# A graph layer with linear attention and a mixture of experts: tokens sent to tiles of their experts, heads computed for two blocks at once, selves and query softmax moved into the first pass, 28 dense sets in place of 12

## The chip, the cores and the metric

The kernel runs on one NeuronCore of one Trainium2 chip. The metric is the device time of one execution in microseconds, the median of several. Engines: TensorE (PE in the profile, PEld its weight loads), VectorE (DVE), ScalarE (ACT), GpSimd (POOL), and the sync engine (SP), which here only issues DMAs.

## The reference

6250 nodes with 256 features, 200,000 edges sorted by destination. `xn` is the layer norm of `x`. Then, per node:

```
neigh = mean of xn[src] over the edges that end at the node
g     = relu([xn, neigh] @ gnn_W + gnn_b); g = g / max(|g|, 1e-12)
q,k,v = xn @ Wqkv, 8 heads of 32; q = softmax over a head's 32 features, k = softmax over all nodes
mix   = layernorm((q * scale) @ (k^T v) @ Wout) * gamma
x     = x + g + mix
tokens = layernorm(x)
x     = x + tokens + sum over the 2 best of 8 experts: weight * (gelu(tokens @ w1[e] + b1[e]) @ w2[e] + b2[e])
```

The two weights are the softmax of the router's logits, scaled to sum to one. All products but the one over the edges are in float32.

## The kernel before

The nodes are 49 blocks of 128 rows. Edges are tiles of 128, and as they are sorted by destination, tile j belongs to nodes near 4j.

**Two ways to sum over edges.** (1) Gathered tiles: GpSimd fetches the 128 source rows of a tile by an indirect DMA (L609) from a table in DRAM that holds each normalized row as two float16 halves, high and low. VectorE compares destination numbers to make a one-hot (L1273), and PE multiplies it by both halves (L653, L655). 16 tiles form a zone of 128 nodes; its sum is copied by ScalarE (L968), turned by PE (L662) and added by VectorE into `sums` (L1363). There is a ring of 24 gathered tiles. (2) Dense sets: a set is 11 groups of two tiles. PE builds, from two one-hots per tile (source row within a block; 11 destinations x 49 blocks, in two halves), a piece of the adjacency matrix (`build_group`, L687); ScalarE copies it out (L979); then PE multiplies the matrix by the table's rows, which are resident in SBUF (`multiply`, L697 and L699: 49 blocks, two matmuls of 121 weight columns each). Before, 12 sets take 264 tiles this way, and 1299 tiles are gathered.

**Stages.** At the start layer norm statistics, the table and the edges' numbers. First pass (`b1`, 49 units): per block the normalized rows are turned, stored to DRAM, and multiplied to keys and values (L761), which go to DRAM; each unit also has 4 gathered tiles and a share of the dense work. Second pass (`b2`): per block the exponentials of the keys and the context sum (L789), 3 gathered tiles, dense work. A bridge of 16 tiles turns the context into one matrix `w_mix`. Main stage: 49 blocks x 8 experts = 392 steps, with 2.6 gathered tiles per step. In a block's eight steps PE does `up` (L867) and `down` (L878) for each expert on all 128 tokens; ScalarE the Gelu (L1039); VectorE adds each expert's output times its combine weight, which is zero for six of eight (L1531). In the same steps the head of the next block runs: `project` (L805, selves and queries), the query softmax (VectorE and ScalarE, L1424 to L1436), `mix` (L832, L835), then on VectorE a chain of small operations (norms, variances, an inverse square root by Newton steps, L1105 to L1115) up to the tokens, then the routing.

**What sets the order.** Each engine's program is written out by hand from one list of units and steps (`plan_b`, `main_steps`); semaphores couple the engines. `use_order` numbers every use of the PSUM bank `turned`, which most stages share, and its uses follow one another. `plan_b` spreads the dense pieces over the units by a cost in microseconds (0.46 per group built, 0.23 per block multiplied) and a budget per unit. SP's queue holds all plain DMAs in program order, GpSimd's queue all gathers.

## Time and profile before

| | |
|---|---|
| timed, median of 3 runs | 1843.76 us (1841.33 to 1844.39) |
| span of the profiled execution | 2433.1 us |
| granted TensorE clock, mean | 0.908 |
| PE / weight loads busy | 76% / 60% |
| DVE / ACT / POOL busy | 50% / 28% / 53% |
| DMA | 251.14 MB, mean 103 GB/s |

The profile has no time of the profiled execution other than its span, which is well above the timed runs. Busy time of PE is the union of matmul records, whose ends are modelled. "Idle before" is the time that an engine stood still ahead of a group of instructions, with what ended it.

### The profile page before, as it was taken

Reading aid. Unit: us, or ns where it says so; the run is one execution under the profiler, and the core shown is the slowest. Engines: PE = TensorE matmul, PEld = TensorE weight load, DVE = VectorE, ACT = ScalarE, POOL = GpSimd, SP = SyncE. Lnnn points to the kernel's source line nnn. Section 1 sums busy time; section 2 is a strip of 40 time slices with the busy share of each in tenths; the row PEclk is TensorE's granted clock in tenths of the full one; section 3 lists DMA queues with packets and bytes.
Section 4 is the critical chain, followed back from the end, with each engine's and each line's share of the span. In section 5 each row is a group of like instructions: output and inputs, shape, how many; then the busy total and the mean of one; then the engine's idle time right before and its main releaser. Section 6 shows DMA issues by size and latency. Waiting matters only on the chain.

```text
span 2433.1 us, 34393 instructions
## 1 busy us (share of the span) xinstructions
PE 1851.1 (76%) x11044; PEld 1449.7 (60%) x11044; DVE 1222.2 (50%) x4533; ACT 685.0 (28%) x1736; POOL 1277.6 (53%) x1310
## 2 busy tenths in 40 slices
PE   0578877878748787787887787877778777777888
PEld 0355555666526665666666666666666666666677
DVE  8322222442235555455555555555555555555576
ACT  6333333332202222222222222222222222222233
POOL 1655565464655654655555555655555555545510
PEclk9899999998868988988989998988998989988999
DMA  7445554443642332322332332332332322322310
GB/s 256 140 147 158 161 158 142 121 118 106 183 120 79 98 94 66 100 77 85 98 89 80 90 94 83 94 89 76 91 92 84 90 85 85 90 81 84 92 42 13
DMA packets 144715, 251.14 MB, mean 103 GB/s; under 512 B 28046, under 2 KB 96062, under 8 KB 144542
## 3 DMA queue, kind: packets, MB, share of 16 engines
q0 software_dynamic: 62352, 170.35, 24.6%
q1 hardware_dynamic: 82190, 78.59, 10.1%
q8 instruction: 95, 1.56, 0.3%
q14 instruction: 78, 0.64, 0.1%
HBM read 216.74 MB, written 32.09 MB: 102 GB/s over the span
## 4 chain that ended last, share of the span: by engine, by line
PE 47%; another core or an unknown queue 22%; DVE 11%; issue 11%; ACT 8%; DMA 1%; SPq 1%; POOL 0%; DVEq 0%; POOLq 0%; ACTq 0%
PE ps_hidden L867 9%; PE ps_expert L878 9%; PE ps_zone L653 3%; PE ps_zone L655 3%; PE ps_proj L832 3%; PE ps_proj L805 2%; PE ps_proj L835 2%; ACT sb_stage L1039 2%; PE ps_zone L697 2%; PE ps_turned L662 2%; PE ps_zone L699 2%; PE ps_hidden L761 2%; PE ps_proj L761 2%; PE ps_expert L687 1%
## 5 line engine op out<-in xcount | busy, mean ns | idle before, releaser
L609 POOL DMA_INDIRECT sb_ring<-xn_table,sb_idx x1299 | 1270.1, 978 | 1050.4 <-PE ps_zone L655 485.3
L878 PE MATMUL ps_expert<-sb_arena,sb_stage 128*128 128x256 f32 x1568 | 444.7, 408 | 61.4 <-DVE sb_arena L1531 34.0
L1039 ACT ACTIVATE sb_stage<-ps_hidden,sb_b_col 128x128 f32<-128x128 f32 x784 | 241.7, 365 | 874.3 <-remote 469.1
L867 PE MATMUL ps_hidden<-sb_arena 128*128 128x128 f32 x3136 | 458.5, 293 | 27.7 <-ACT sb_stage L1039 21.0
L867 PEld LDWEIGHTS ps_hidden<-sb_arena 128*128 128x128 f32 x3136 | 415.8, 206 | 64.6 <-issue 30.7
L1531 DVE SCALAR_TENSOR_TENSOR sb_arena<-ps_expert,sb_small,sb_arena 128x256 f32<-128x256 f32 x392 | 189.0, 482 | 337.1 <-remote 211.6
L653 PE MATMUL ps_zone<-sb_ring,sb_onehot 128*128 128x256 f16 x1299 | 336.6, 287 | 22.6 <-issue 12.4
L878 PEld LDWEIGHTS ps_expert<-sb_arena,sb_stage 128*128 128x128 f32 x1568 | 287.4, 204 | 99.5 <-issue 58.3
L655 PE MATMUL ps_zone<-sb_ring,sb_onehot 128*128 128x257 f16 x1299 | 337.1, 288 | 6.2 <-issue 6.2
L655 PEld LDWEIGHTS ps_zone<-sb_ring,sb_onehot 128*128 128x128 f16 x1299 | 133.5, 103 | 62.6 <-issue 19.3
L653 PEld LDWEIGHTS ps_zone<-sb_ring,sb_onehot 128*128 128x128 f16 x1299 | 134.6, 104 | 51.5 <-issue 14.5
L697 PE MATMUL ps_zone<-sb_arena,sb_adjacency 128*121 128x256 f16 x588 | 147.0, 288 | 15.3 <-issue 10.9
L1273 DVE TENSOR_TENSOR sb_onehot<-sb_iota,sb_rel 128x512 f16<-128x512 f16 (+1 forms) x325 | 136.4, 420 | 34.2 <-PE ps_zone L655 24.6
L699 PE MATMUL ps_zone<-sb_arena,sb_adjacency 128*121 128x257 f16 x588 | 146.2, 287 | 9.3 <-issue 9.2
L832 PE MATMUL ps_proj<-sb_w_nb,sb_sums 128*128 128x256 f32 x196 | 77.7, 536 | 95.7 <-ACT sb_stage L1029 87.6
L832 PEld LDWEIGHTS ps_proj<-sb_w_nb,sb_sums 128*128 128x128 f32 x196 | 45.6, 257 | 112.3 <-ACT sb_stage L1029 96.4
L697 PEld LDWEIGHTS ps_zone<-sb_arena,sb_adjacency 128*121 128x121 f16 x588 | 84.3, 143 | 32.4 <-issue 25.7
L1363 DVE TENSOR_TENSOR sb_sums<-ps_turned,sb_sums 128x256 f32<-128x256 f32 x82 | 34.4, 419 | 133.9 <-PE ps_turned L662 105.6
L805 PE MATMUL ps_proj<-sb_w_aq,sb_arena 128*128 128x512 f32 x196 | 97.2, 620 | 0.0
L699 PEld LDWEIGHTS ps_zone<-sb_arena,sb_adjacency 128*121 128x121 f16 x588 | 84.3, 143 | 15.8 <-issue 15.6
L662 PE MATMUL ps_turned<-sb_consts,sb_arena 128*128 128x128 f32 x196 | 39.4, 283 | 70.1 <-DVE sb_arena L1436 35.2
L662 PEld LDWEIGHTS ps_turned<-sb_consts,sb_arena 128*128 128x128 f32 x196 | 25.6, 143 | 108.6 <-issue 55.7
(175 smaller groups left out, 2267.8 us busy)
## 6 DMA issues: line engine op xcount, KB each, us to landing
sb_ring<-xn_table,sb_idx POOLq DMA_INDIRECT x1299
keys_values<-sb_stage SPq DMA_DIRECT2D x49, 256.0 KB
sb_stage<-keys_values SPq DMA_DIRECT2D x96, 128.0 KB
sb_sums<-x SPq DMA_DIRECT2D x7, 896.0 KB, 11.1
sb_stage<-x SPq DMA_DIRECT2D x49, 128.0 KB
xn_transposed<-sb_stage SPq DMA_DIRECT2D x49, 128.0 KB
sb_arena<-xn_transposed SPq DMA_DIRECT2D x49, 128.0 KB
sb_arena<-x SPq DMA_DIRECT2D x49, 128.0 KB
```

Of the source, the lines that this page charges most:

```text
L609: pool.indirect_dma_start(ring3[:, place, 0:2 * D], None, table, bass.IndirectOffsetOnAxis(tile_idx, 0)).then_inc(signal, 16)
L653: pe.matmul(zone_bank(z)[:, 0:D], oh, rows[:, 0:D], start=first, stop=False, skip_group_check=True)
L655: pe.matmul(zone_bank(z)[:, 0:D + 1], oh, rows[:, D:2 * D + 1], start=False, stop=last, skip_group_check=True).then_inc(tiles_used, 1)
L697: pe.matmul(set_sum[0:SET_ROWS, 0:D], adj3[:, h, :], rows16[:, h, 0:D], start=h == 0, stop=False, skip_group_check=True)
L699: mm = pe.matmul(set_sum[0:SET_ROWS, 0:D + 1], adj3[:, h, :], rows16[:, h, D:2 * D + 1], start=False, stop=h == BLOCKS - 1, skip_group_che ...
L805: mm = pe.matmul(proj[:, :], halves(xnt[b % 2])[:, c, :], w_aq3[:, c, :], start=c == 0, stop=c == KC - 1)
L832: pe.matmul(proj[:, 0:D], sums3[:, c, sum_col(b * P):sum_col(b * P) + P], w_nb3[:, c, :], start=c == 0, stop=c == KC - 1, skip_group_check ...
L867: mm = pe.matmul(hidden[e % 2][:, j * P:(j + 1) * P], w1_sb[:, e, c, j * P:(j + 1) * P], halves(tokens_t[b % 2])[:, c, :], start=c == 0, s ...
L878: mm = pe.matmul(expert[e % 2][:, 0:D], halves(act_h[e % len(act_h)])[:, c, :], w2_sb[:, e, c, :], start=c == 0, stop=c == KC - 1, skip_gr ...
L1039: ins = act.activation(halves(act_h[e % len(act_h)])[:, j, :], hidden[e % 2][:, j * P:(j + 1) * P], ACT.Gelu, bias=b1_col[:, e * KC + j:e ...
L1273: return dve.tensor_tensor(to.rearrange("p t (c two) -> p t c two", two=2), numbers.rearrange("p (c two) -> p c two", two=2).unsqueeze(1). ...
L1531: dve.scalar_tensor_tensor(out=out_sb[b % 2], in0=expert[e % 2][:, 0:D], scalar=combine[b % 2][:, e:e + 1], in1=out_sb[b % 2], op0=ALU.mul ...
```

## The change

- `SETS` 12 to 28: 616 tiles are dense, 947 gathered. Budgets and tiles per unit change: `B1_TILES, B2_TILES` 4, 3 to 6, 8; `B1_DENSE, B2_DENSE` 2.1, 2.7 to 3.6, 6.9. The zones use one PSUM bank throughout.
- Selves and queries (`selves_queries`) and the query softmax (`split_projection`, `exp_q`, `soften_q`) run in the first pass; the turned soft queries and the selves go to DRAM (`queries_selves`) in place of the transposed rows.
- Heads run for a pair of blocks in 8 steps (25 pairs, 200 steps, 1.4 gathered tiles per step), most VectorE operations on both blocks at once.
- The experts no longer run on every token. Blocks form cohorts of 14, 12, 10, 8 and 5. When a cohort's logits are there, VectorE picks two experts per token (`choose`), PE counts ranks (`rank`), and VectorE finds each token's row in a buffer in which every expert's tokens fill whole tiles of 128 (`dispatch`). GpSimd scatters each block's tokens twice by an indirect DMA (`scatter`). A cohort of n blocks has 2n + 7 jobs, 133 in all, whatever the routing; a job loads its expert's weights (number read by SP from SBUF), b2 and 128 tokens, computes, and stores its answer. Later GpSimd fetches each block's two answers (`fetch_answers`), and VectorE adds them to the block's base row (`finish`).
- The sent buffers are cleared by DMA in the first pass; the weights are first copied in DRAM into one pack per expert. After the 200 head steps 50 more steps hold the last 36 jobs and the last sums; the first job is in step 90.

```diff
-SETS = 12
+SETS = 28
-OH_RING = 16
+OH_RING = 20
-B1_TILES, B2_TILES = 4, 3
-B1_DENSE, B2_DENSE = 2.1, 2.7
+B1_TILES, B2_TILES = 6, 8
+B1_DENSE, B2_DENSE = 3.6, 6.9
-HEAD0_TILES = (4, 4, 8)
-MAIN_RATE = 2.6
+HEAD0_TILES = (8, 8)
+SLOTS = 8
+MAIN_RATE = 1.4
+W_BUFS, T_BUFS = 5, 4
+COHORTS = (14, 12, 10, 8, 5)
+JOBS_OF = [2 * n + EXPERTS - 1 for n in COHORTS]
...
             for u in B1_UNITS:
                 turn(("xn", u.block), xn_b).then_inc(turn_filled, 1)
                 dense(u.before)
                 sum_tiles(u.tiles)
+                if u.block:
+                    turn_q(u.block - 1)
                 keys_values(u.block)
+                selves_queries(u.block)
                 dense(u.after)
                 turn_zones(u.tiles)
...
+            def load_job(n):
+                g = max(c for c in range(len(COHORTS)) if JOB_FIRST[c] <= n)
...
+                e = sp.value_load(owner[0:1, n:n + 1], min_val=0, max_val=EXPERTS - 1)
+                wait(sp, expert_filled, n - W_BUFS + 1)
+                sp.dma_start(w_bufs[n % W_BUFS], pack[bass.ds(e * P, P), :]).then_inc(w_landed[n % W_BUFS], 16)
+                wait(sp, expert_filled, n - T_BUFS + 1)
+                sp.dma_start(b2_bufs[n % T_BUFS], b2[bass.ds(e, 1), :]).then_inc(b2_landed[n % T_BUFS], 16)
+                wait(sp, sent_turned, n - T_BUFS + 1)
+                row = (n - JOB_FIRST[g]) * P
+                sp.dma_start(sent_in[n % T_BUFS], sent[g][row:row + P, :]).then_inc(sent_landed[n % T_BUFS], 16)
+            def store_answer(n):
+                sp.wait_ge(y_copied, n + 1)
...
+                sp.dma_start(answers[g][row:row + P, :], y_out[n % 2]).then_inc(y_stored[n % 2], 16)
...
+                for n in st.stores:
+                    store_answer(n)
+                for n in st.ticks:
...
+                    if n + 1 < JOBS:
+                        load_job(n + 1)
+                for b in st.loads:
+                    load_base(b)
...
+            def scatter(b, choice):
...
+                pool.indirect_dma_start(sent[COHORT[b]], bass.IndirectOffsetOnAxis(row_of[:, choice, b:b + 1], 0),
+                                        tokens[b % TOKEN_RING], None
+                                        ).then_inc(scattered[b // 2 % TOKEN_PAIRS], 16)
...
+            def down(n):
+                pe.wait_ge(hidden_act, n + 1)
+                wait(pe, y_copied, n - 1)
+                for c in range(KC):
+                    pe.matmul(expert[n % 2][:, 0:D], halves(act_h[n % 2])[:, c, :], w2_of[n % W_BUFS][:, c, :],
+                              start=c == 0, stop=False, skip_group_check=True)
+                row = 32 * (n % T_BUFS)
+                pe.wait_ge(b2_landed[n % T_BUFS], n // T_BUFS * 16 + 16)
+                pe.matmul(expert[n % 2][:, 0:D], ones[row:row + 1, :], b2_bufs[n % T_BUFS], start=False, stop=True,
+                          skip_group_check=True).then_inc(expert_filled, 1)
+            def tick(n):
+                if n < JOBS:
+                    turn_sent(n)
+                if 1 <= n <= JOBS:
+                    up(n - 1)
+                if n >= 2:
+                    down(n - 2)
...
+            for st in STEPS:
+                sum_tiles(st.tiles)
+                if st.part == 1 and st.pair + 1 < PAIRS:
+                    count_degrees(st.pair + 1)
+                    mix(st.pair + 1)
+                for g in st.rank:
+                    rank(g)
+                for n in st.ticks:
+                    tick(n)
+                if st.part == 4:
+                    turn_tokens(st.pair)
+                if st.part == 6:
+                    route(st.pair)
+                turn_zones(st.tiles)
```

## Rows read from the trace of the kernel before

**Rows 1.** The page: the span; the chain that ended last, by engine.
```profile
span 2433.1 us, 34393 instructions
...
PE 47%; another core or an unknown queue 22%; DVE 11%; issue 11%; ACT 8%; DMA 1%; SPq 1%; POOL 0%; DVEq 0%; POOLq 0%; ACTq 0%
```
**Rows 2.** Waits: who waited for whom, us in total, times, longest us.
```profile
ACT sb_stage L1039 <- remote: 469.1, 89, 9.4
```
**Rows 3.** Windows: busy us (count) of PE, PEld, DVE, ACT, POOL; clock, DMA share, GB/s.
```profile
0.00:75.80 75.80, 10.90 (x47) 7.60 (x48) 62.59 (x195) 47.87 (x65) 14.84 (x17) 1.00 0.73 235
75.80:430.00 354.20, 273.97 (x1595) 185.74 (x1594) 98.44 (x205) 117.77 (x296) 211.85 (x211) 0.94 0.50 150
430.00:686.50 256.50, 192.10 (x1389) 157.76 (x1389) 89.37 (x190) 66.28 (x190) 144.25 (x137) 0.87 0.47 138
686.50:2341.00 1654.50, 1293.42 (x7522) 1031.43 (x7521) 910.83 (x3695) 419.45 (x1095) 906.65 (x946) 0.90 0.30 87
2341.00:2433.00 92.00, 80.66 (x498) 67.20 (x496) 61.01 (x249) 33.67 (x90) 0.00 (x0) 0.99 0.04 13
```
**Rows 4.** Timeline of PE at 1295 us and 1315 us: start, duration, what.
```profile
1295.17 1.88 PE L805 MATMUL ps_proj<-sb_w_aq,sb_arena 128*128 128x512 f32 x4
1297.10 0.27 PE L653 MATMUL ps_zone<-sb_ring,sb_onehot 128*128 128x256 f16 x1
1297.21 0.28 PE L655 MATMUL ps_zone<-sb_ring,sb_onehot 128*128 128x257 f16 x1
...
1315.58 1.06 PE L867 MATMUL ps_hidden<-sb_arena 128*128 128x128 f32 x8
1316.48 1.03 PE L878 MATMUL ps_expert<-sb_arena,sb_stage 128*128 128x256 f32 x4
```
**Rows 5.** Timeline of GpSimd: gathers that wait for nothing, and a slow one.
```profile
1250.02 0.95 POOL L609 DMA_INDIRECT sb_ring<-xn_table,sb_idx  x1 [0.31 <-issue]
1251.27 0.94 POOL L609 DMA_INDIRECT sb_ring<-xn_table,sb_idx  x1 [0.30 <-issue]
...
502.39 2.03 POOL L609 DMA_INDIRECT sb_ring<-xn_table,sb_idx  x1 [0.30 <-issue]
```
**Rows 6.** Groups of weight loads: count, busy us, mean ns, idle before.
```profile
L653 PEld LDWEIGHTS ps_zone<-sb_ring,sb_onehot 128*128 128x128 f16 x1299 | 134.6, 104 | 51.5 <-issue 14.5 <-ACT sb_zone_sb L968 7.8 <-DMA sb_ring<-xn_table,sb_idx 5.7
L697 PEld LDWEIGHTS ps_zone<-sb_arena,sb_adjacency 128*121 128x121 f16 x588 | 84.3, 143 | 32.4 <-issue 25.7 <-ACT sb_adjacency L979 6.7
```
**Rows 7.** Groups of VectorE: the two comparisons for four dense tiles.
```profile
L1273 DVE TENSOR_TENSOR sb_key_onehot<-sb_iota_key,sb_rel 128x2160 f16<-128x2160 f16 x66 | 84.3, 1277 | 0.0
L1273 DVE TENSOR_TENSOR sb_lo_onehot<-sb_iota,sb_lo_pairs 128x512 f16<-128x512 f16 x66 | 28.1, 425 | 104.5 <-PE ps_expert L687 68.5 <-PE ps_hidden L687 23.9 <-remote 9.7
```
**Rows 8.** Groups of VectorE: operations of the heads.
```profile
L1455 DVE SCALAR_TENSOR_TENSOR sb_arena<-ps_proj,sb_small,sb_gamma_row 128x256 f32<-128x256 f32 x49 | 23.7, 484 | 1.7
L1452 DVE BATCH_NORM_STATS2 sb_small<-ps_proj 128x6 f32<-128x256 f32 x49 | 20.6, 421 | 0.0
L1111 DVE SCALAR_TENSOR_TENSOR sb_small<-sb_small 128x1 f32<-128x1 f32 x441 | 84.2, 219 | 10.4
L1115 DVE SCALAR_TENSOR_TENSOR sb_small<-sb_small 128x1 f32<-128x1 f32 x441 | 57.5, 158 | 10.0
```
**Rows 9.** DMA queues (packets, MB, share of 16 engines) and issues (KB, us to landing).
```profile
q1 hardware_dynamic: 82190, 78.59, 10.1%
...
sb_sums<-x SPq DMA_DIRECT2D x7, 896.0 KB, 11.1
...
xn_table<-sb_arena SPq DMA_DIRECT2D x3, 896.0 KB, 5.6
```
**Rows 10.** A register load, and SP's issues on the timeline.
```profile
L956 ACTq TENSOR_LOAD <-sb_flag x1: 1029/1029/1029, 59.3 to 59.3; - x1
...
59.60 1.97 SPq L514 DMA_DIRECT2D sb_stage<-x  x2
...
1417.77 0.46 SPq L542 DMA_DIRECT2D sb_arena<-x  x1
```

More of the change, by code:

```diff
@@ L574, in _ @@
+            for b in late:
+                store_out(b)
             for n in (0, 1):
@@ L1615, in constants @@
+                add_zones(st.tiles)
 def constants():
```

1057 lines of the change are left out of this document (642 added, 415 removed).

## The prediction

> **What bounds the kernel now.** The page comes first, and its span doesn't fit the runs: 2433.1 us profiled, 1843.76 us timed (median) [rows 1]. The chain of waits gives 22% of the span (535 us) to "another core or an unknown queue", on a kernel that has one core. The waits on ScalarE say where: 89 times it sat up to 9.4 us in front of the Gelu with no releaser known, 469.1 us in all [rows 2]; the matmuls it waited for had long ended, and PE ran on until it was itself blocked. 535 us is nearly the 589 us that separate the profile from the runs, so I take these stalls as the profile's own and work with busy intervals and with the distance between neighbouring starts, which they don't touch.
>
> Two engines are near their limit. GpSimd starts a gather every 1.25 us when nothing stops it [rows 5], and has 1299: 1628 us. It starts them at 73 us and has none left in the last 92 us [rows 3], 80 of them without the stalls: 73 + 1628 + 80 = 1781 us, 97% of the timed 1844. PE at full clock: neighbouring starts are 0.11 us apart for a 256-column f16 matmul, 0.90 us for the eight of an `up` (L867), 0.86 for the four of a `down` (L878) and 1.72 for four 512-column ones (records of 1.03 and 1.88 less the 0.16 or 0.17 by which a record outlasts its slot) [rows 4]. With the counts: ups 392 x 0.90 = 353, downs 392 x 0.86 = 337, gathered tiles 1299 x 0.22 = 286, dense sets 1176 x 0.11 = 129, keys/values and selves/queries 98 x 1.72 = 169, mixes 49 x 1.72 = 84, builds 132 x 0.47 = 62, and 143 for turns, routing, bias and context: 1563 us. So both GpSimd and PE bound the kernel, and the kernel runs 1.035 times above the larger one. In the main stage (686 us on) GpSimd and PE are evenly matched; VectorE is at 55%, the DMA engines at 30% [rows 3].
>
> **The change, part by part.** The profiled span is 2433; the sums below are stall-free ones, to be held against 1844, and the profile of the changed kernel should again lie some 500 us above its runs (the stalls come with PE's instructions, which fall by a tenth).
>
> *Experts.* Each of 392 (block, expert) pairs becomes one of 133 fixed tile jobs. A job on PE: two transposes 0.22, up 0.90, down 0.86, one-row b2 matmul 0.43 (two at 0.215, as in `down`) = 2.41 us, so 321 us in place of 353 + 337 + 31 (bias): -400 us of PE.
>
> *Dense sets, 12 to 28.* Gathers fall from 1299 to 947: -441 us of GpSimd, -77 of PE. PE gains 16 x 98 x 0.11 = 172 and 176 builds x 0.47 = 83. The rest of PE's work only moves. PE's sum is 1340 us, GpSimd's 947 gathers + 98 scatters + 98 answer fetches, 1143 x 1.25 = 1429 us. The trace has no scatter; I price it as a gather. It could cost 0.95 us (a gather's record without the gap) or 2.0 us (the record of a slow gather) [rows 5]: -30 to +75 us of GpSimd work, on the path only if GpSimd is, which it isn't after the second pass.
> The weights of a set are 121 columns wide, and their loads take 143 ns against 104 for 128 columns [rows 6]. The Trainium skill's page "TensorE: Matmul & The Clock Gate", section on weight-path modes, has the rule: fast weight load wants exactly 128 weights that are not FP32. If loads set the pace, 2744 of them would add 91 us. But the set's matmuls also start 0.11 us apart, so the sum stays.
>
> *Start.* 17 copies of the weights into the pack are issued by SP ahead of the first block's load; SP's DMA issues take 0.46 us, two early ones 1.97 [rows 10]; at 0.5 us +9 us, the first pass starts at 85 instead of 76 us. Bounds: 0 if SP were early, 26 if their 8.4 MB hold up the first loads at the 320 GB/s of [rows 9].
>
> *First pass (49 blocks, now 6 tiles each).* PE per block: transposes 0.44, keys/values 1.72, selves and queries 1.72, tiles 1.32, dense 3.6, zone turn 0.1: 8.9 us, 436 in all. GpSimd needs 7.5, VectorE about 6. The query softmax is a chain PE, VectorE 1.3, ScalarE 0.4, VectorE 1.1, and PE takes its result 5.4 us of its own work later: hidden; without that cover it costs up to 1.5 us per block. The builds are not paced by PE: four tiles of one-hots cost VectorE 0.42 + 1.28 [rows 7], a set has 5.5 such batches, 9.4 us against 5.2 on PE plus some 2 to 3 us of gathered tiles between. That is up to 2.5 us per set; half of it for 11 sets, +14. Stage: 450.
>
> *Second pass and bridge.* 8 tiles per block are 10.0 us of GpSimd against 9.2 of PE for 44 blocks. 392 + 16 gathers x 1.25 = 510, less the 24 of the ring's lead (30) = 480. PE, 405 + 42 for builds, hides under it. Stage: 481. These two passes take the place of 611 profiled us [rows 3], some 470 stall-free.
>
> *Heads, 90 steps before the first job (11.25 pairs).* VectorE sets this: per pair 8 scalar_tensor_tensor x 0.48, 4 statistics x 0.42, 2 squares x 0.5, 2 x 512 columns at 0.65, 2 x 0.45, and 32 tiny chained operations at 0.16 to 0.22 plus a gap of 0.035 [rows 8]: 15.2; with one-hots 1.2, zones 0.4 and waits 18.2 us. PE has 7.4, GpSimd 14 plus scatters. 205 us.
>
> *Heads with jobs, 110 steps, 99 jobs.* PE: 99 x 2.41 = 239, heads 67, tiles 27: 333 us. DMA: a job moves 0.79 MB (its weights anew, tokens, answer): 78 MB; 120 gathers, 60 scatters and 52 fetches 30 MB, heads, base rows and out 21: 130 MB, at 320 GB/s (78.59 MB in 10.1% of the span) 405 us [rows 9]. SP: each job has a register load of 1.03 us and four issues [rows 10], 2.9 us; 330 in all. Bounds 333 and 405; I take the middle, 370, because a job's weights come in packets of 4 KB, larger than that queue's.
>
> *Tail.* 36 jobs with no head work: PE 2.4, SP 3.3, DMA 1.05 MB = 3.3 us; 3.6 each, 130, and 25 for the last cohort's fetches and sums: 155 us. Below 36 x 3.0 + 20 = 128; above, see the first rival.
>
> Sum: 85 + 1.035 x (450 + 481 + 205 + 370 + 155) = 85 + 1719 = **1804 us**, 2.2% under 1844: 222 us less PE work is mostly lost because no two stages are bound by the same engine, and PE idles in the early heads and in the tail.
>
> **Rivals.** *1. The job loop is late (slower).* SP issues job n+1 only after it has stored the answer of n-3, in one queue with the heads' loads; PE then waits for 525 KB. Landings in the trace were 11.1 us for 896 KB and 5.6 for another 896 KB [rows 9], that is 3.3 to 6.5 us per 525 KB. For it: SP's 2.9 us stand ahead. Against: five weight buffers. It decides once a tick takes over 4.0 us. At 4.6 us: 99 x 4.6 = 455 in place of 370, tail 191 in place of 155, x 1.035: 1929 us.
> The Trainium skill's page "DMA: Bandwidth & Descriptors", in its section on the anatomy of one DMA (GpSimd's path), fits 2.0 us plus bytes / 436e3; by that estimate a job's weights land in 3.2 us, which is below 4.0 and speaks against this rival; no run here shows it yet.
> *2. Every stage runs at PE's or GpSimd's floor (faster).* Start 80, 436, 481, 205, 333, 128: 80 + 1.02 x 1583 = 1695 us. For it: the timed kernel before is within 3.5% of such a floor. Against: that was one long stage with steady lead; here six follow each other.
> *3. One-hots pace the builds in both passes.* 3.1 us per set: +20 in the first pass, +30 in the second, where it shows past GpSimd: about 1855 us. For it: in the trace a set's builds take 10 us at best where PE needs 5.2.
> *That the change doesn't do what it says:* the jobs are a fixed 133 whatever the routing, so their number can't fail; the branch for far edges would cost milliseconds, but with 28 sets no edge of this input lies outside its window. No chance is given to it.
>
> **How the numbers follow.** Forecast 0.40 (own range 1750 to 1850, about a tenth of it not under 1840), rival 2 0.27, rival 1 0.18, rival 3 0.15. A measurement of this kernel tells 0.2%, 4 us. Faster: 0.27 + 0.34 + 0.02 = 0.63; within: 0.04; slower: 0.18 + 0.13 + 0.02 = 0.33. The range is 1680 to 1940: it leaves out the parts of rivals 1 and 2 that run further.
>
> **What would show it.** First pass near 9.2 us per block, second near 10.2 with GpSimd gathering every 1.25 us without a break; from the second pass's end a stretch of some 205 us with VectorE over 85% busy and PE under half; then jobs at a DMA share over 0.8; last some 36 jobs 3.6 us apart. Wrong, if jobs stand over 4.0 us apart and PE waits for weights (rival 1), if builds wait for VectorE's one-hots (rival 3), or if a scatter holds GpSimd far over 2 us.

## The result and the profile after

The changed kernel takes **2242.02 us** (median of 4 runs, 2236.48 to 2246.38), the kernel before 1843.26 us beside it (1841.33 to 1844.39): a ratio of 1.217, 95% interval 1.214 to 1.219. The forecast was 1804 us, the range 1680 to 1940. Both were wrong, and so was the sign.

The span of the profiled execution is 2237.5 us and fits the runs; the stalls "another core or an unknown queue" of [rows 1, 2] are absent. First the page's span and chain, then a table of windows cut near the stages' ends (busy us of PE, PEld, DVE, ACT, POOL; clock, DMA share, GB/s), which answers [rows 3]:

```profile
span 2237.5 us, 31285 instructions
...
PE 51%; DVE 14%; DMA 11%; SPq 6%; POOL 6%; ACT 5%; issue 5%; DVEq 0%; POOLq 0%; ACTq 0%
```
```profile
0.00:128.00 128.00, 17.98 (x89) 15.31 (x90) 70.35 (x198) 48.99 (x69) 34.58 (x35) 1.00 0.80 194
128.00:690.00 562.00, 481.13 (x2755) 323.48 (x2753) 256.58 (x608) 197.09 (x505) 291.88 (x288) 0.95 0.50 156
690.00:1215.00 525.00, 453.66 (x3618) 366.78 (x3617) 221.00 (x443) 155.33 (x466) 406.21 (x380) 0.95 0.42 121
1215.00:1467.00 252.00, 156.16 (x734) 120.79 (x734) 176.57 (x717) 13.80 (x44) 175.84 (x180) 0.67 0.47 142
1467.00:1930.00 463.00, 377.26 (x1957) 286.98 (x1958) 198.38 (x795) 126.83 (x369) 194.98 (x199) 0.83 0.72 231
1930.00:2237.00 307.00, 202.81 (x881) 151.75 (x879) 46.93 (x149) 74.61 (x217) 70.32 (x73) 0.77 0.62 194
```

Only in the two passes is PE over 85% busy. In the early heads (fourth line) no engine is: PE 62%, VectorE 70%, GpSimd 70%, the clock at 0.67. In the last two nothing is full either: DMA 0.72 and 0.62, PE 81% and 66%. The stages, cut at the first keys/values matmul, the first of the context, the first mix, the first turn of sent tokens (L1097) and the last mix, stand against the forecast's terms (each with its 1.035) like this:

| us | start | first pass | second pass, bridge | early heads | jobs beside heads, and tail |
|---|---|---|---|---|---|
| forecast | 85 | 466 | 498 | 212 | 543 |
| changed kernel | 128 | 566 | 539 | 238 | 458 + 308 |

The first four errors are 43, 100, 41 and 26 us, the last 223.

The early heads are two things. Twelve pairs begin 16.4 us apart (from 1233 to 1430 us, by the first VectorE operation of each). Then PE stands still for 31.3 us before the first job, because the first cohort's tokens are not all sent: its 28 scatters stand among 38 gathers in GpSimd's queue, 1.29 us for each, and take from 1379 to 1464 us. The last of them, and PE's first turn of sent tokens:

```profile
1463.35 0.99 POOL L822 DMA_INDIRECT sent_tokens<-sb_arena  x1 [0.30 <-issue]
```
```profile
1471.44 0.69 PE L1097 MATMUL ps_hidden<-sb_consts,sb_stage 128*128 128x128 f32 x2 [31.30 <-DMA sb_stage<-sent_tokens]
```

The largest wait on PE (its longest piece is that one), and where the start was lost (engine, line, what it waited for, us, times, longest):

```profile
PE ps_hidden L1097 <- DMA sb_stage<-sent_tokens: 186.2, 71, 31.3
...
ACT sb_stage L1224 <- DMA sb_stage<-x: 52.8, 1, 52.8
```

What lands last for PE is not the 513 KB of weights but the 128 KB of tokens, which are issued behind them. The chain of waits in the tail (start us, us, what) shows how one turn of the job loop runs:

```profile
2102.93 0.69 PE ps_hidden L1097 x2
2103.62 1.71 PE ps_hidden L1108 x8
2105.33 1.33 PE ps_expert L1118 x4
2106.66 0.64 PE ps_expert L1122 x2
2107.32 0.39 ACT sb_stage L1306
2107.73 0.33 SPq L712
...
2108.11 0.46 SPq L699
...
2109.55 0.29 SPq L703
...
2109.89 3.56 DMA sb_stage<-sent_tokens
...
2113.50 0.69 PE ps_hidden L1097 x2
```

It is a ring. PE ends tick n, ScalarE copies the answer, SP stores it, and only then issues the loads of job n+2, whose tokens are the first thing that tick n+2 wants. From L1097 at 2102.93 to L1097 two ticks later at 2113.50 are 10.6 us; over the 54 jobs that end behind the last mix a tick takes 5.16 on average. PE has been idle for 3.15 us when the first of these two ticks begins; the granted clock is 0.5 from 2102.74 to 2106.15 us (`up` 1.71 us) and then 1.0, also in the second tick, which the chain doesn't show (its `up` has a record of 1.06, as in [rows 4]). The page's landings (KB each, us from issue to landing):

```profile
sb_adjacency<-expert_pack SPq DMA_DIRECT2D x54, 513.0 KB, 4.1
...
sb_stage<-sent_tokens SPq DMA_DIRECT2D x133, 128.0 KB, 3.9
```

### The profile page after: what moved, and what is told of

Read it like the earlier page. It is cut to its first block, busy times and chain, and to the rows that moved or that the text cites. A ratio compares the mean times of both kernels' runs of the same rounds, so it can differ in the third digit from the quotient of the medians.

```text
span 2237.5 us, 31285 instructions
## 1 busy us (share of the span) xinstructions
PE 1689.0 (75%) x10026; PEld 1265.1 (57%) x10026; DVE 969.8 (43%) x2909; ACT 616.7 (28%) x1669; POOL 1173.8 (52%) x1154
## 4 chain that ended last, share of the span: by engine, by line
PE 51%; DVE 14%; DMA 11%; SPq 6%; POOL 6%; ACT 5%; issue 5%; DVEq 0%; POOLq 0%; ACTq 0%
DMA sb_stage<-sent_tokens 9%; PE ps_zone L913 7%; PE ps_zone L915 7%; PE ps_hidden L1108 5%; POOL sb_ring L789 5%; PE ps_expert L1118 5%; PE ps_proj L977 4%; PE ps_hidden L984 4%; DVE sb_key_onehot L1519 4%; PE ps_zone L869 3%; PE ps_zone L871 3%; PE ps_expert L1122 3%; PE ps_expert L903 2%; ACT sb_adjacency L1213 2%; PE ps_hidden L1097 2%
## 5 line engine op out<-in xcount | busy, mean ns | idle before, releaser
L789 POOL DMA_INDIRECT sb_ring<-xn_table,sb_idx x947 | 970.6, 1025 | 669.4 <-PE ps_zone L871 347.4
L913 PE MATMUL ps_zone<-sb_arena,sb_adjacency 128*121 128x256 f16 x1372 | 313.5, 274 | 4.9 <-ACT sb_adjacency L1213 4.8
L915 PE MATMUL ps_zone<-sb_arena,sb_adjacency 128*121 128x257 f16 x1372 | 312.7, 274 | 0.0
L869 PE MATMUL ps_zone<-sb_ring,sb_onehot 128*128 128x256 f16 x947 | 260.3, 303 | 54.4 <-DMA sb_ring<-xn_table,sb_idx 33.9
L837 POOL DMA_INDIRECT sb_stage<-answers,sb_arena x98 | 94.0, 959 | 282.7 <-DVE sb_arena L1860 167.6
L1097 PE MATMUL ps_hidden<-sb_consts,sb_stage 128*128 128x128 f32 x266 | 69.2, 351 | 186.4 <-DMA sb_stage<-sent_tokens 186.2
L1519 DVE TENSOR_TENSOR sb_key_onehot<-sb_iota_key,sb_rel 128x2160 f16<-128x2160 f16 x154 | 196.6, 1276 | 0.0
L913 PEld LDWEIGHTS ps_zone<-sb_arena,sb_adjacency 128*121 128x121 f16 x1372 | 185.3, 135 | 18.4 <-ACT sb_adjacency L1213 11.9
L915 PEld LDWEIGHTS ps_zone<-sb_arena,sb_adjacency 128*121 128x121 f16 x1372 | 185.7, 135 | 7.9 <-issue 7.9
L903 PE MATMUL ps_expert<-sb_key_onehot,sb_lo_onehot 128*128 128x275 f16 (+1 forms) x820 | 151.5, 293 | 32.9 <-ACT sb_adjacency L1213 16.9
L1213 ACT ACTIVATE sb_adjacency<-ps_expert 128x275 f16<-128x275 f32 (+1 forms) x410 | 154.9, 418 | 70.9 <-PE ps_expert L903 70.0
L1097 PEld LDWEIGHTS ps_hidden<-sb_consts,sb_stage 128*128 128x128 f32 x266 | 34.4, 167 | 220.8 <-DMA sb_stage<-sent_tokens 214.8
L822 POOL DMA_INDIRECT sent_tokens<-sb_arena x98 | 98.3, 1003 | 98.2 <-DVE sb_arena L1844 69.9
```

The source lines that it names most:

```text
L789: pool.indirect_dma_start(ring3[:, place, 0:2 * D], None, table, bass.IndirectOffsetOnAxis(tile_idx, 0)).then_inc(signal, 16)
L822: pool.indirect_dma_start(sent[COHORT[b]], bass.IndirectOffsetOnAxis(row_of[:, choice, b:b + 1], 0), tokens[b % TOKEN_RING], None).then_in ...
L869: pe.matmul(zone_bank[:, 0:D], oh, rows[:, 0:D], start=first, stop=False, skip_group_check=True)
L903: mm = pe.matmul(build[q % BUILD_BUFS][:, 0:keys.stop - keys.start], lo_onehot3[:, place, :], key_onehot3[:, place, keys], start=n == 0, s ...
L913: pe.matmul(set_sum[0:SET_ROWS, 0:D], adj3[:, h, :], rows16[:, h, 0:D], start=h == 0, stop=False, skip_group_check=True)
L915: mm = pe.matmul(set_sum[0:SET_ROWS, 0:D + 1], adj3[:, h, :], rows16[:, h, D:2 * D + 1], start=False, stop=h == BLOCKS - 1, skip_group_che ...
```

## The experiments on the job loop

**e1, a longer lead.** Undoes the ring: job n+2 is loaded where n+1 was, with buffers for it.

```diff
-W_BUFS, T_BUFS = 5, 4
+W_BUFS, T_BUFS = 5, 7
-                    if n + 1 < JOBS:
-                        load_job(n + 1)
+                    if n + 2 < JOBS:
+                        load_job(n + 2)
```


> Job n+2 is loaded in tick n in place of job n+1, with seven buffers for tokens and b2 in place of four, so that the loads have one more tick (about 5.2 us) to land. Theory A (the job loop is a ring: answer stored, next job's loads issued 1.5 us later, tokens landed 3.2 to 4.6 us later, then PE; two ticks per turn, 10.3 us): the wait for sent_tokens, 102 us in the heads with jobs and 62 us in the tail of the changed kernel, goes, and part of the low clock with it; a tick falls from 5.2 to about 3.7 to 4.2 us and the kernel takes 2040 to 2110 us. Theory B (the DMA engines are full: 378 MB, 0.72 busy in the heads with jobs, 0.60 in the tail): an earlier issue brings nothing, 2225 to 2245 us, and the landings grow by a tick.

Measured: 2073.03 us (2063.03 to 2080.56), ratio 1.123 (1.119 to 1.128): 169 us less. Theory A holds, B falls: the same 378.5 MB now move at 286 in place of 231 GB/s, and a pack lands in 5.2 us in place of 4.1, which no longer matters. The tail's tick fell from 5.16 to 3.85 us. The DMA share is 0.87 and 0.78 now; whether bandwidth is the next limit no run tested. Jobs beside heads and the tail, of this kernel:

```profile
1471.00:1844.00 373.00, 333.93 (x1957) 255.66 (x1955) 198.81 (x792) 126.23 (x369) 191.22 (x195) 0.91 0.87 286
1844.00:2079.00 235.00, 173.22 (x881) 126.01 (x879) 47.41 (x153) 74.07 (x217) 70.25 (x73) 0.85 0.78 250
```

**e2, tokens ahead of the weights** in `load_job` (the three lines of `sent_turned`, `row` and `sent_in` moved to its top).


> Within a job's loads the 128 KB of tokens are issued first, ahead of the register load, the 513 KB of weights and b2. Theory A: the tokens are issued 1.0 us earlier and no longer queue behind the weights, so they land in about 2.5 us in place of 3.9; the ring of two ticks is 2 to 2.4 us shorter, the tick 4.1 to 4.3 us, the kernel 2100 to 2150 us. Theory B: the same bytes in the same time, 2230 to 2245 us.

Measured: 2114.67 us (2112.80 to 2131.82), ratio 1.151 (1.145 to 1.157), tick 4.23 us. The time is A's, 127 us less at the same bytes, but the way is only half of A's: the tokens don't land sooner after their issue, 4.3 us (median) in place of 3.9. What leaves the ring is the time between the store and the issue of the tokens. In the chain above it is 1.8 us (2108.06 to 2109.89), for the register load and two other issues; here it is 0.05 (medians over the tails: 1.84 and 0.04):

```profile
2008.52 0.35 SPq L712 DMA_DIRECT2D answers<-sb_stage  x1
2008.92 0.42 SPq L701 DMA_DIRECT2D sb_stage<-sent_tokens  x1
```
```profile
sb_stage<-sent_tokens SPq DMA_DIRECT2D x133, 128.0 KB, 4.3
```

1.8 us in two ticks are about the 0.93 us by which the tick fell.

**e3, weights loaded once** (five whole packs, then 8 columns of each; later jobs compute with stale weights).

```diff
-                sp.dma_start(w_bufs[n % W_BUFS], pack[bass.ds(e * P, P), :])...
+                cols = slice(0, PACK) if n < W_BUFS else slice(0, 8)
+                sp.dma_start(w_bufs[n % W_BUFS][:, cols], pack[bass.ds(e * P, P), cols])...
```


> Leaves out the weight traffic: only the first five jobs load whole packs, the later ones 8 of 1026 columns (the jobs then compute with the wrong weights). 67 of 378 MB are gone. Theory B: DMA time falls by 67 MB at 230 to 320 GB/s, 210 to 290 us of it in the jobs' stages, and the kernel takes 1950 to 2050 us; the DMA share in the tail falls under 0.3 and the tick to PE's 3.0. Theory A: the tokens no longer land behind 513 KB, so they take about 2.5 us in place of 3.9, as in the run with the tokens first: 2100 to 2170 us, and not below that run by more than 1%.

Measured: 2125.75 us (2119.38 to 2127.60), ratio 1.153 (1.149 to 1.156). The tokens land in 2.1 us in place of 3.9 and the DMA share of the tail is 0.41, and yet this is no faster than e2, which moves all the weights. So the changed kernel doesn't run into full DMA engines. What the weights' bytes cost it is 1.8 us of landing in a turn of the ring, as much as e2 takes out of the turn in another place. The tail of e3 as a window, and its landing of tokens:

```profile
1867.00:2126.00 259.00, 189.94 (x881) 136.97 (x879) 46.92 (x149) 75.19 (x217) 70.90 (x73) 0.80 0.41 125
```
```profile
sb_stage<-sent_tokens SPq DMA_DIRECT2D x133, 128.0 KB, 2.1
```

**e4, PE kept busy while it waits** (14 matmuls ahead of `turn_sent`, from tick 97 on).


> In the last 36 jobs, without head work beside them, PE runs 14 extra float16 matmuls of 256 columns (1.5 us at full clock) ahead of each tick's turn, where it waits for the tokens. If the low clock (0.76 in the tail; 39 of its 247 us) makes PE's part of the ring long, the turn, the up and the down take 2.0 us in place of 3.6 and the tail falls by 25 to 60 us: 2180 to 2217 us. If only the landing of the tokens sets the tick (theory A alone, the PE part hidden) or DMA bandwidth does (B), nothing or the extra work's cost: 2238 to 2270 us.

Measured: 2221.41 us (2209.93 to 2228.03), ratio 1.204 (1.198 to 1.210): 21 us less, just short of the 25 to 60 that were expected. The tail's clock rose from 0.77 to 0.89 and its tick fell from 5.16 to 4.90 us. So the low clock is a part of the ring, a small one.

## The experiments on the start, the passes and the heads

All on top of e1 (2073 us).

**e5, the copies into the pack issued inside the first pass** (two per second block).


> On top of the longer lead (2073 us): the 16 copies of weights into the pack, 8.4 MB, are issued two at a time in every second block of the first pass, and no longer ahead of the first block's load. Theory: in the changed kernel ScalarE waited 52.8 us for the first x load behind them, and the first pass began at 128 us in place of 85; it now begins at 80 to 90 us and the kernel takes 2030 to 2040 us. Rival: the copies only move their cost into the first pass, whose own loads and stores they now delay (DMA share there 0.50): the first pass grows by 20 us or more, 2055 to 2075 us.

Measured: 2033.06 us (2020.37 to 2040.45), ratio 1.103 (1.097 to 1.109). 40 us less; the first pass begins at 83 us and is as long as it was (567 us). The start is settled.

**e6, the wide comparison left out** behind the first batches (the dense sums come from stale one-hots).

```diff
-                compare(key_onehot3[:, place:place + DOH_BATCH, :], iota_key[:, :], ..., KEY_COLS)
+                cols = KEY_COLS if t < DOH_RING else 16
+                compare(key_onehot3[:, place:place + DOH_BATCH, 0:cols], iota_key[:, 0:cols], ..., cols)
```


> On top of the longer lead (2073 us). Leaves out most of the one-hots of the dense tiles' keys: after the first two batches the comparison of 2160 columns covers 16 x 4 columns (the dense sums then come from stale one-hots). 152 comparisons of 1.28 us are gone from VectorE, 190 us over the two passes. If the one-hots pace the builds (rival 3 of the prediction), directly and by holding up the zone sums and the softmax queued behind them (23 + 4 us and 27 + 15 us of PE's idle time in the two passes), 50 to 75 us: 2000 to 2025 us. If VectorE is beside the path, and PE waits for ScalarE's evictions and for gathers instead, 5 to 30 us: 2043 to 2068 us.

Measured: 2003.32 us (1998.46 to 2016.96), ratio 1.090 (1.084 to 1.095): first pass 528 in place of 567, second 505 in place of 539. It is worth 70 us, though PE's waits for these one-hots were only 20 (e1). A part of the way is GpSimd's. Its timeline in the changed kernel's second pass, and VectorE's below it (start us, us, what):

```profile
916.11 0.94 POOL L789 DMA_INDIRECT sb_ring<-xn_table,sb_idx  x1 [0.30 <-issue]
917.35 1.80 POOL L789 DMA_INDIRECT sb_ring<-xn_table,sb_idx  x1 [0.30 <-issue]
919.46 0.95 POOL L789 DMA_INDIRECT sb_ring<-xn_table,sb_idx  x1 [0.31 <-PE ps_zone L871]
920.71 1.98 POOL L789 DMA_INDIRECT sb_ring<-xn_table,sb_idx  x1 [0.30 <-issue]
```
```profile
917.06 1.28 DVE L1519 TENSOR_TENSOR sb_key_onehot<-sb_iota_key,sb_rel 128x2160 f16<-128x2160 f16 x1
...
920.60 1.28 DVE L1519 TENSOR_TENSOR sb_key_onehot<-sb_iota_key,sb_rel 128x2160 f16<-128x2160 f16 x1
```

The gathers at 917.35 and 920.71 begin while a wide comparison has 0.99 and 1.17 us to run, and take 0.85 and 1.03 us more than the 0.95 of the others. Counted over the second pass: 376 gathers, of which 130 overlap a wide comparison and take 1.29 us on average, the other 246 take 0.96; of 86 over 1.2 us, 84 overlap one. In e6's second pass there is no such comparison and 5 gathers are over 1.2 us; the gathers start 1.29 us apart in place of 1.38, which over 376 of them is 34 us, all that this pass gained. In the first pass, where GpSimd waits for PE much of the time, the way of the 39 us is not shown. The groups of gathers, in the changed kernel and in e6 (count, busy us, mean ns):

```profile
L789 POOL DMA_INDIRECT sb_ring<-xn_table,sb_idx x947 | 970.6, 1025 | 669.4 <-PE ps_zone L871 347.4 <-issue 263.7 <-DVE sb_ring L1559 58.4
```
```profile
L791 POOL DMA_INDIRECT sb_ring<-xn_table,sb_idx x947 | 916.1, 967 | 588.3 <-issue 266.2 <-PE ps_zone L873 264.2 <-DVE sb_ring L1560 57.8
```

The Trainium skill's page "SBUF — State Buffer", in its section on SBUF's two separate sides, says that VectorE and GpSimd share one pair of ports, that VectorE takes it in certain fast modes or with two inputs in SBUF (then only against a GpSimd operation that reads SBUF), that whoever holds it has it for the whole instruction, and that GpSimd can't write the descriptors of its DMAs while VectorE holds it in such a mode. The trace agrees in that a gather is held up by nearly what is left of the comparison; that the port does it, no run here shows.

**e9, ScalarE's copies of the built pieces cut** to 22 of 264 or 275 columns, from the second set on (which leaves stale columns in the matrices).


> On top of the longer lead (2073 us). Leaves out most of the copies of the built adjacency pieces: from the second set on ScalarE copies 22 columns of each half in place of 264 or 275 (the later sets then multiply partly stale pieces). 594 copies of 0.42 us fall to some 0.2. PE waited 30 us in the first pass and 21 in the second for these copies, and leaving out VectorE's comparison brought 70 us, more than its own waits: both engines serve a build, ScalarE 0.84 us a group (two halves), VectorE 0.85. If ScalarE paces the builds as VectorE does, 25 to 70 us: 2003 to 2048 us. If the comparison alone paced them and ScalarE's waits only pass it on, 0 to 20 us: 2053 to 2075 us.

Measured: 2069.04 us (2062.93 to 2083.61), ratio 1.125 (1.120 to 1.131), nothing that can be told from e1. Of PE's 51 us of waits for ScalarE in e1's passes 27 are for these copies; in e9's second pass they go (4 us to 0) and the waits for the wide one-hots grow from 18 to 28, in the first they stay (22 and 19).

**e7, 20 dense sets.** `SETS` 20, `B2_TILES` 7, budgets 2.6 and 4.9, `MAIN_RATE` 2.7.


> On top of the longer lead (2073 us): 20 dense sets in place of 28, 1123 gathered tiles in place of 947 (6 and 7 per block in the passes, 2.7 per step in the heads), dense budgets 2.6 and 4.9 in place of 3.6 and 6.9. By the summed slots 8 sets are 8 x (98 x 0.11 + 11 x 0.47) = 128 us of PE, gone from the passes, and 49 tiles less in the second; the heads gain 225 tiles, 50 us of PE and 280 us of GpSimd. If the passes are paced by PE and what it waits for, they fall from 1106 to 960 to 990 us, the early heads grow from 238 to 300 (243 gathers and scatters at 1.25) and the heads with jobs by 20 to 50: 2000 to 2060 us. If 28 sets are the better balance, 2075 to 2120 us.

Measured: 2131.41 us (2130.55 to 2140.26), ratio 1.158 (1.154 to 1.163), slower, and above both ranges that were expected. The passes fell as expected (507 and 464 us), but the early heads took 362 us in place of 238 and the heads with jobs 440 in place of 373: GpSimd is 76% busy in the first of these, and PE waits 110 us there for gathers.

**e8, six cohorts** (10, 10, 10, 8, 6, 5) in place of 14, 12, 10, 8, 5.


> On top of the longer lead (2073 us): cohorts of 10, 10, 10, 8, 6 and 5 blocks in place of 14, 12, 10, 8 and 5, so 140 jobs in place of 133, and the first job some 22 steps earlier. If what is lost behind the passes is that the early heads leave PE and the DMA engines idle (PE slots 92 of 238 us) and the jobs come after, the early heads fall by about 55 us, the tail from 54 jobs to about 40 (-50 us), and the heads with jobs grow by 30 to 60: 2020 to 2050 us. If jobs and heads cannot run beside each other (VectorE's chain per pair delayed by each other's waits, DMA share already 0.8), 2065 to 2110 us.

Measured: 2070.65 us (2061.12 to 2077.77), ratio 1.125 (1.120 to 1.130), the same. Early heads 175 in place of 238, tail 208 in place of 235, and 445 in place of 373 between: the time moved with the work.

**e10, all together.** e1, e2 and e5; besides, PE's gathered tiles stand between its dense pieces, and the turn of the soft queries behind `selves_queries`.

```diff
             for u in B1_UNITS:
...
-                dense(u.before)
-                sum_tiles(u.tiles)
-                if u.block:
-                    turn_q(u.block - 1)
+                dense(u.before, u.tiles)
                 keys_values(u.block)
                 selves_queries(u.block)
+                if u.block:
+                    turn_q(u.block - 1)
```


> The whole computation: longer lead, tokens ahead of weights, copies of the weights inside the first pass (2033 us for the lead and the copies), and two reorderings on PE: the gathered tiles of a unit are spread between its first dense pieces, so that PE has other work while ScalarE and VectorE serve a build, and the turn of the soft queries stands behind selves_queries, with two buffers. If PE's idle time in the passes (110 and 111 us) is a matter of order, some 40 to 80 us of it go, and another 10 to 25 us in the jobs: 1930 to 1985 us. If ScalarE and VectorE are near their own limit in a unit, reordering moves the waits only: 2000 to 2030 us. Neither reaches the kernel before (1842).

Measured: 1966.57 us (1964.41 to 1969.62), ratio 1.068 (1.066 to 1.071). The first pass fell by 35 us and the second by 13; 276 us below the changed kernel, 126 above the one before. The start gave 43 us of the 106 since e1; the jobs beside the heads gave 12 and the tail 6.

**e11, no jobs at all.**


> On top of the longer lead (2073 us). Leaves out the experts' work altogether: no job is loaded, computed or stored; tokens are still chosen, ranked and scattered, and the fetches read the sent tokens in place of answers. What is left is the two passes, 25 pairs of heads and the sums. By the stages of the longer lead's trace: 1232 us to the first mix, 25 pairs at the 21 us that a pair takes before the first job (238 us for 11.25), 525, and 30 behind them: 1750 to 1800 us, so the experts' jobs add about 290 us beside and behind the heads. If a pair is slowed by nothing but jobs and could run at VectorE's 15 us, 1640 to 1690 us.

Measured: 1879.84 us (1875.32 to 1884.18), ratio 1.021 (1.018 to 1.024). Without any of the experts' products the changed kernel is still 2% slower than the kernel before with all of them. The 24 pairs between the first and the last mix take 21.4 us on average, but not evenly: the first 13 stand 17.6 us apart (1234 to 1463 us), near VectorE's 15.2 with its one-hots and zones, the next 11 stand 27 us apart, with scatters and fetches beside them, and VectorE waits 63 us there for fetched rows. What exceeds the expectation are the 130 us behind the last mix: GpSimd has 81 instructions there, 21 scatters and 60 fetches (30 blocks), and VectorE waits 62 us for fetched rows; the plan puts the fetches behind the jobs' steps. Heads and rest:

```profile
1234.00:1748.00 514.00, 291.12 (x1375) 223.81 (x1376) 365.13 (x1474) 29.08 (x91) 350.07 (x357) 0.66 0.48 148
1748.00:1878.00 130.00, 7.03 (x30) 5.19 (x28) 53.50 (x177) 1.55 (x5) 79.62 (x81) 0.51 0.47 147
```

## The experiments on the kernel before

**e12, the same kernel, profiled again.**


> The kernel before, unchanged, profiled again. If the 469 us for which ScalarE stood in front of the Gelu with no releaser known belong to that one profiled execution, this one's span is 1840 to 1900 us, and its stages can be laid beside those of the changed kernel: first pass 330 to 350 us, second 235 to 250, main stage 1170 to 1200. If profiling this program always brings them, the span is 2300 to 2500 us again.

Measured: 1843.67 us (one run), span 1841.6, as expected if the stalls belong to that one execution. The stages are not as expected: the passes are shorter (290 and 209 us) and the main stage longer (1267). Without the stalls of the first profile, the page's busy line and the windows of start, passes and main stage are:

```profile
PE 1656.9 (90%) x11044; PEld 1333.5 (72%) x11044; DVE 1216.6 (66%) x4533; ACT 692.9 (38%) x1736; POOL 1275.3 (69%) x1310
```
```profile
0.00:75.70 75.70, 10.91 (x47) 7.58 (x48) 62.59 (x195) 47.83 (x65) 15.01 (x17) 1.00 0.72 235
75.70:365.70 290.00, 260.83 (x1618) 181.96 (x1618) 104.17 (x221) 119.86 (x304) 215.98 (x211) 0.98 0.62 187
365.70:575.00 209.30, 178.54 (x1423) 151.85 (x1422) 92.80 (x211) 63.27 (x185) 148.85 (x146) 0.94 0.58 171
575.00:1841.60 1266.60, 1206.59 (x7960) 992.09 (x7960) 957.01 (x3909) 461.99 (x1182) 895.43 (x938) 0.99 0.39 113
```

For 1267 us the main stage has PE 95% busy at a clock of 0.99, with the heads, the experts and the gathers beside each other. That is what the change took apart.

**e13, 28 sets and nothing else** (4 and 8 tiles per block, budgets 3.6 and 8.1, one tile per step; the numbers of the edges moved to where after has them, as they need room).


> The kernel before with 28 dense sets and nothing else of the change: 4 and 8 gathered tiles per block in the passes in place of 4 and 3, dense budgets 3.6 and 8.1, one tile per step in the main stage. Theory (PE bounds the kernel before: 90% busy at a clock of 0.986 in its second profile, GpSimd 69%): 16 sets more are +172 us of multiplies and +83 of builds, 352 gathered tiles less -77; in the passes the work added (255 of sets, 54 of tiles) takes 1.3 times its slots, +400, the main stage loses 597 tiles, -131 and no more: 2050 to 2150 us. Rival (what the prediction held: GpSimd bounds it, at 1628 us of gathers, and 441 us of it go): the main stage, freed of gathers, gives back more than the passes take: 1750 to 1840 us.

Measured: 2166.39 us (2164.36 to 2168.40), ratio 1.175 (1.171 to 1.178). The dense sets alone cost 322 us, a little above what was expected. Its windows answer to the last three above:

```profile
81.00:456.50 375.50, 342.06 (x2289) 248.81 (x2288) 143.67 (x282) 151.78 (x402) 219.91 (x211) 0.98 0.48 145
456.50:1017.00 560.50, 473.40 (x3632) 371.68 (x3630) 225.06 (x452) 155.71 (x466) 400.61 (x389) 0.92 0.41 121
1017.00:2164.00 1147.00, 1080.14 (x6695) 876.25 (x6693) 892.17 (x3695) 447.11 (x1145) 324.77 (x343) 0.99 0.19 57
```

The main stage lost 597 gathered tiles, 750 us of GpSimd's time, and got 120 us shorter, PE's 131 for those tiles. The passes grew by 437 us for 309 us of new slots.

**e14, 16 sets** (budgets 2.5 and 3.9, rate 2.3).


> The kernel before with 16 dense sets in place of 12: dense budgets 2.5 and 3.9, 2.3 gathered tiles per step in place of 2.6. If PE bounds the kernel: +43 +21 -19 = +45 us of PE, 1.1 to 1.3 times in the passes, 1885 to 1925 us. If GpSimd bounds it: 88 gathers less, 110 us of GpSimd, of which PE lets some 20 to 50 through: 1790 to 1835 us.

Measured: 1891.00 us (1887.74 to 1892.03), ratio 1.025 (1.022 to 1.027): 47 us for 45 us of PE's work; 110 us off GpSimd are worth nothing. The waits of e12 say why: PE waits for gathers 19 us in all, and by this trace that is the most that a faster GpSimd could give.

```profile
POOL sb_ring L609 <- PE ps_zone L655: 41.7, 52, 14.9
```
```profile
PE ps_zone L653 <- DMA sb_ring<-xn_table,sb_idx: 18.8, 28, 1.6
```

The first line is the other side: GpSimd waits for PE only 42 us. It runs its 1299 gathers from 67 to 1755 us, 1.30 us apart, so that 69% busy is nearly its full pace. PE bounds the kernel before, and GpSimd is close behind; what less work for PE alone would give was not run.

## The search for a better version

**e15**, e10 with six cohorts.


> The whole computation: all of the run together (1967 us) and cohorts of 10, 10, 10, 8, 6 and 5 blocks. On the longer lead alone these cohorts brought 2 us (2071 against 2073): the early heads fell by 63 us and the tail by 27, and the heads with jobs grew by 72. With the tokens ahead of the weights the jobs may stand closer beside the heads: 1935 to 1955 us. If the jobs' own time (140 at 4.5 us) is what counts wherever they stand, 1960 to 1975 us. No version of this kernel is then under the one before.

Measured: 1960.38 us (1950.60 to 1967.95), ratio 1.061 (1.057 to 1.065). It is the fastest version of the changed kernel by its median (its runs overlap with those of e10), 282 us below it and 117 above the kernel before. The time is the one expected if the jobs cost the same wherever they stand. PE still stands 25 us before the first job.

**e16 and e17**, e15 with 24 sets (rate 1.9) and with 20 (rate 2.35).


> As the run with everything together and six cohorts (1960 us), with 24 dense sets in place of 28, 1.9 gathered tiles per step, dense budgets 3.1 and 5.9. Four sets are 4 x 15.9 = 64 us of PE slots and 83 us of the passes at 1.3. The early heads gather 125 tiles in 66 steps, 1.25 each with 20 scatters: 180 us, as now. The heads with jobs get 67 tiles more, 15 us of PE and 84 of GpSimd, which has slack there (445 us for 134 steps, now 190 gathers and 140 scatters and fetches, 410 us): 30 to 70 us longer. Theory (a set costs 12 to 20 us): 1905 to 1940 us. Rival (GpSimd takes over at once): 1955 to 1990 us.

> As before with 20 dense sets, 2.35 gathered tiles per step, dense budgets 2.6 and 4.9. The passes lose 127 us of slots, 165 us at 1.3; GpSimd has 155 gathers and 20 scatters in 66 early steps (220 us, +43) and some 270 gathers and 140 scatters and fetches in the heads with jobs (512 us and more, +90 to +130). Theory: about even with 24 sets, 1920 to 1960 us. Rival (as with the longer lead alone, where 20 sets cost 58 us): 2000 to 2030 us.

Measured: 1986.76 us (1986.07 to 1992.30), ratio 1.077 (1.073 to 1.081), and 2057.37 us (2048.99 to 2063.57), ratio 1.115 (1.110 to 1.120). Both theories of e16 and e17 that counted on PE missed; the rival of e16 holds, and e17 is 27 us above its own:

| us | first pass | second, bridge | early heads | jobs beside heads | tail |
|---|---|---|---|---|---|
| e15, 28 sets | 533 | 527 | 177 | 441 | 204 |
| e16, 24 sets | 503 | 525 | 203 | 478 | 201 |
| e17, 20 sets | 490 | 519 | 239 | 528 | 201 |
| e18, 24 sets, 8 and 8 tiles | 538 | 531 | 174 | 437 | 200 |

The second pass hardly feels its sets (527, 525 and 519 us): its 408 gathers set it.

**e18**, e16 with `B1_TILES` 8, budgets 2.9 and 6.1 and 1.3 tiles per step.


> As the run with 24 sets (1987 us), but the 98 gathered tiles that two more per block make go into the first pass (8 and 8 tiles per block, dense budgets 2.9 and 6.1) and out of the heads (1.3 per step in place of 1.9). Theory (a pass takes the longer of PE's slots times 1.2 to 1.3 and GpSimd's 10 us per block): first pass 49 x 10.0 to 10.4 = 490 to 510 us, second 520, as now; the heads fall back to those of 28 sets or below, 177 and 441 in place of 203 and 478: 1915 to 1935 us. Rival (more gathers in the first pass collide with its stores, loads and copies of weights, DMA share 0.6, and the gain is given back): 1950 to 1980 us. Either is over the 1842 of the kernel before.

Measured: 1967.84 us (1966.49 to 1969.54), ratio 1.067 (1.065 to 1.069). The heads fell as expected, the first pass did not: 538 us for 392 gathers. The time is in the rival's range, but not for its reason alone: in both passes GpSimd's gathers stand 1.35 us apart on average, where the sum has 1.25, and most of this is the wide comparison again. In the first pass 73 gathers overlap one and take 1.38 us in place of 0.97, in the second 119 take 1.23 in place of 0.96: 30 and 32 us. This is the row of the first pass, with GpSimd at 77%:

```profile
84.00:622.00 538.00, 457.35 (x2683) 311.61 (x2682) 250.68 (x621) 184.83 (x472) 416.32 (x400) 0.97 0.69 200
```

## Why the prediction was wrong

Three steps failed: the reading that work taken from GpSimd pays, the factor 1.035 on the passes, and, with 223 of the 433 us the largest, the pricing of the job loop by what PE, SP and DMA can do per job and not by the ring that couples them.

- **"Both GpSimd and PE bound the kernel."** PE did (e12 to e14), with GpSimd close behind. GpSimd's path of 1781 us, the larger of the two sums, was rightly read as running at its own pace, but PE was late by its own work and its idle time, and waited only 19 us for gathers. The 441 us that the change took from GpSimd were worth nothing that shows, and the +178 us of PE for sets, which the prediction had in its sum, cost 322 in e13.
- **PE's sum for the changed kernel, 1340 us,** nearly held: slots of PE taken from neighbouring starts at full clock add up to some 1370 us, and 26 of the 30 us more are the one-row b2 matmuls, 0.31 us each and not 0.215. What was missed lies beside it, as idle time behind the start (some 500 us) and as low clock (some 200 us, both added up over PE's records).
- **The factor 1.035** is the step that failed in the passes. It was the kernel's whole time over its larger sum, and the main stage's in essence. The passes of the kernel before had some 400 us of slots in 499 us, 1.25 (e12), those of e13 721 in 936, 1.30, and those of the changed kernel some 828 in 1087, 1.31. On the prediction's own sums for PE, 436 and 405 us, 1.25 gives 1051 us and 1.31 gives 1102; measured were 1105 with the bridge. [rows 3] hinted at it, with the stalls of that profile in it: 466 us of PE records in 611 us.
- **First pass, 450.** Its parts held (436 of PE, measured some 433). Rival 3, one-hots that pace the builds, was right in kind: e6 shows 39 us there and 34 in the second pass. Its way was only half seen: a wide comparison also holds up the gathers.
- **Second pass, 481,** was rightly GpSimd's, at 1.38 us per gather and not 1.25; the 130 gathers beside a wide comparison make 43 us of it. [rows 5] showed the slow gather of 2.03 us and the prediction set it aside.
- **Start, 85.** The bound of 26 us for the pack's 8.4 MB was too low and the value below it; they cost 43 (e5).
- **Early heads, 205,** measured 238. The price of a pair was right, even high: 16.4 us, not 18.2. What the sum left out is the 31 us for which PE stands in front of the first job while GpSimd still sends the first cohort. That the order of scatters and gathers in GpSimd's queue does it is read from the trace; no run changed it. VectorE's time per pair lies open here; in the kernel before it ran beside the experts' matmuls.
- **Jobs, 370, and tail, 155.** Rival 1 came true and beyond its price: 5.2 us a tick against 4.6. Its condition was met ("once a tick takes over 4.0 us"), but what lands last are not the weights but the tokens behind them. The step that failed is the middle between two rates, 333 us for PE and 405 for DMA: the tick is half a turn of a ring of landing, PE, copy, store and SP's issues, 10.6 us, and part of PE's share of it runs at half clock. Taking the tokens' issue forward by a tick (e1) gives 169 us back. With a lead of two ticks the heads with jobs took 373 us, as forecast, but 79 jobs had ended by the last mix where the prediction counted 99 by the end of the heads' steps, and the other 54 took 3.85 us each in place of 3.6. The fit that the prediction cites from the Trainium skill's page "DMA: Bandwidth & Descriptors" (section on the anatomy of one DMA) gives, as an estimate, 2.3 us for the 128 KB of tokens, though it is fitted on GpSimd's path and the tokens go by SP's queue. e3 is near it with 2.1 us; the changed kernel's 3.9 are not, nor are the 4.3 of e2, where the tokens are issued ahead of their own job's weights. So it is the weights' bytes in flight that lengthen the landing, not the place in the order.

In sum, by the runs: dense sets +322 (e13, alone). On top of them, the experts as jobs, the paired heads and the moved softmax cost 76 more (2242 against 2166); with the job loop, the start and PE's order mended (e15) they gain 206. No single cause is enough: with those mended the kernel still takes 1960 us with its 28 sets, and fewer sets on top make it slower (e16, e17). Not tested are the scatters ahead of the gathers in GpSimd's queue, fetches earlier than behind the jobs' steps, and whether DMA bandwidth limits the mended job loop (share 0.87 in e15). What a kernel with 12 sets and jobs would take was not run: its 1299 gathers, 98 scatters and 98 fetches would be 1869 us of GpSimd at 1.25 each, an estimate from [rows 5], above the kernel before. That is the change's bind: fewer sets are too many gathers, more sets too much PE in passes where PE is at 1.3 times its slots.

Open stays what makes up the rest of the passes' idle time (in e6 PE is idle some 75 of 528 and some 75 of 483 us, counted from its slots).

## What to carry to other kernels

Find which engine bounds by changing its load a little, as with 4 sets more, before taking sums near each other for a tie: work off the other engine is worth no more than the bounding one waits for it. The busy share doesn't tell: GpSimd at 69% was near its full pace. Take the factor of time over slots stage by stage: a long even stage with PE 95% busy hides what runs beside it, and what is taken out of it costs its own time. In a loop where a load is issued only after a result is stored, write down the ring and its lead before pricing bandwidth, and issue the load that is needed first right behind the store. Where one stage hands a whole group to the next, look for what else stands in the queue that delivers it.

## What the hardware showed

- A gather issued by GpSimd takes 0.96 us, and 1.29 on average while VectorE runs a 2160-column float16 comparison of 1.28 us (130 of 376 in the second pass).
- 128 KB land in 2.1 us when 8 of a pack's 1026 columns are loaded ahead of them (e3), in 3.9 us behind a whole pack of 513 KB, and in 4.3 us when they are issued first and the pack of the job before is under way (e2).
- A matmul with one row of weights and 256 float32 columns takes 0.31 us at full clock, one with 128 rows 0.22 (spacing of neighbouring starts in the changed kernel's jobs, L1122 and L1118).
- One profiled execution was 32% longer than the runs, by stalls of which the second profile of the same kernel has none; PE's granted clock was 0.908 in it and 0.986 in the second. The prediction's guess that they don't belong to the kernel was right; its guess that the changed kernel's profile would have them too was wrong.
- 14 extra matmuls per tick made the tail faster (clock 0.77 to 0.89, tick 5.16 to 4.90 us).
